# A decoder layer: shared expert cut at 384 and 320, and the output norm on ScalarE

## The reference

```python
yg = xf @ shared_gw.T
y, g = jnp.split(yg, 2, axis=-1)          # 704 hidden columns each
shared = jax.nn.silu(g) * y @ shared_dw.T
...
for e in range(N_EXPERTS):                # 8 experts, 352 hidden columns, top 2
    h = jax.nn.silu(g_e) * u_e
    out = out + h @ down_w[e].T * we[:, None]
x = _layernorm(x + shared + out)
```

## Time and profile before

| what | value |
|---|---|
| median of 3 runs | 1037.55 us (1037.47 to 1037.67) |
| the profiled execution | 1038.49 us |
| its span | 1036.8 us |
| PE busy | 1010.6 us, 97% of the span |
| DVE busy | 748.6 us, 72% |
| ACT, POOL busy | 566.4 us, 581.7 us |
| mean granted clock of TensorE | 0.998 |

### The profile page before, as it was taken

How to read it: one execution, slowest core, us unless ns; L and a number is a source line. 1 busy time by engine, 2 the same in 40 slices (tenths; PEclk the granted TensorE clock), 3 DMA queues, 4 the chain that set the end, 5 groups by cost and what they waited for, 6 DMA issues and landing times.

```text
span 1036.8 us, 20483 instructions
## 1 busy us (share of the span) xinstructions
PE 1010.6 (97%) x6817; PEld 905.3 (87%) x6817; DVE 748.6 (72%) x1567; ACT 566.4 (55%) x1221; POOL 581.7 (56%) x565
## 2 busy tenths in 40 slices
PE   8999999999999999999999999999999999999997
PEld 8866678999999999999999999999887888888885
DVE  4268876767767777777776776776786567789857
ACT  5355555655555565555555655555653347777610
POOL 1157777754744754744745745745564545555553
PEclk9999999999999999999999999999999999999999
DMA  8100104324333323233233233234220779999743
GB/s 283 82 22 12 61 22 156 147 115 152 120 110 113 105 107 115 100 111 116 97 114 112 98 119 105 97 125 134 102 89 2 272 281 387 402 403 403 296 122 112
DMA packets 45275, 153.48 MB, mean 148 GB/s; under 512 B 3768, under 2 KB 4792, under 8 KB 42144
## 3 DMA queue, kind: packets, MB, share of 16 engines
q1 hardware_dynamic: 42976, 145.38, 38.7%
q0 software_dynamic: 2240, 7.34, 2.2%
HBM read 130.04 MB, written 22.66 MB: 147 GB/s over the span
## 4 chain that ended last, share of the span: by engine, by line
PE 63%; POOL 8%; issue 5%; DVE 5%; ACT 2%; DMA 1%; POOLq 0%; DVEq 0%; ACTq 0%; SPq 0%
PE xa_y_ps L86 5%; PE xa_y_ps L88 5%; PE xa_y_ps L87 5%; PE xa_turn_ps L2123 3%; PE xa_turn_ps L2167 3%; PE ex_raw_gu_ps L86 3%; PE ex_raw_gu_ps L88 3%; PE ex_raw_gu_ps L87 3%; PE front_k_ps L86 3%; PE front_k_ps L88 3%; PE front_k_ps L87 3%; PE xa_turn_ps L2065 2%; PE xa_scores_ps L2153 2%; PE xa_scores_ps L2149 2%; PE ex_raw_ey_ps L2313 2%
## 5 line engine op out<-in xcount | busy, mean ns | idle before, releaser
L1646 DVE TENSOR_TENSOR xa_kT_lo<-xa_turn_ps,xa_kT_hi 128x750 fp32r<-128x750 f32 x63 | 59.1, 939 | 100.0 <-ACT xa_kT_hi L1427 100.0
L1326 POOL TENSOR_TENSOR xa_probs<-xa_probs,xa_inv_sum 112x750 f32<-112x750 f32 x63 | 94.8, 1505 | 63.3 <-DVE xa_inv_sum L1697 63.3
L1309 POOL TENSOR_TENSOR k_ms<-k_ss,sum_eps 125x6 f32<-125x6 f32 x63 | 12.6, 200 | 160.8 <-DVE k_ss L1662 160.8
L1443 ACT CAST xa_probsT<-xa_turn_ps 125x672 fp32r<-125x672 f32 x62 | 44.6, 720 | 86.4 <-PE xa_turn_ps L2167 86.4
L1312 POOL TENSOR_TENSOR k_inv<-k_ms,neg_half 125x6 f32<-125x6 f32 x63 | 83.6, 1328 | 8.3 <-POOL k_ms L1309 6.7
L1449 ACT ACTIVATE xa_probs<-xa_scores_ps,xa_bias,xa_q_scale 112x375 f32<-112x375 f32 x126 | 82.8, 662 | 7.0 <-DVE xa_bias L1672 5.5
L86 PE MATMUL front_k_ps<-land_xa_wk_hi,land_xa_ctx 128*125 128x256 f32 x252 | 71.8, 285 | 2.2 <-DVE front_k_hat L1689 1.8
L87 PE MATMUL front_k_ps<-land_xa_wk_hi,land_xa_ctx 128*125 128x256 f32 x252 | 70.8, 281 | 0.0
L88 PE MATMUL front_k_ps<-land_xa_wk_lo,land_xa_ctx 128*125 128x256 f32 x252 | 70.8, 281 | 0.0
L1423 ACT ACTIVATE front_k_sq<-front_k_ps 125x512 f32<-125x512 f32 x63 | 37.7, 599 | 60.2 <-PE front_k_ps L88 58.6
L423 POOL TENSOR_TENSOR sa_masked<-sa_masked,sa_row_max 112x448 f32<-112x448 f32 x32 | 30.2, 945 | 60.9 <-DVE sa_row_max L653 60.4
(11 more groups left out here) (445 smaller groups left out, 3703.6 us busy)
## 6 DMA issues: line engine op xcount, KB each, us to landing
xa_nat<-ctx_split SPq DMA_DIRECT2D x56, 750.0 KB
ex_raw_raw<-in_w_units SPq DMA_DIRECT2D x15, 1408.0 KB, 8.2
ex_raw_raw<-in_w_units SPq DMA_DIRECT2D x15, 768.0 KB, 8.1
land_ex_raw<-in_w_units SPq DMA_DIRECT2D x8, 1408.0 KB, 8.0
land_ex_raw<-in_w_units SPq DMA_DIRECT2D x8, 768.0 KB, 8.2
ctx_split<-xa_nat SPq DMA_DIRECT2D x8, 750.0 KB
sorted_x<-ex_raw_y_sb SPq DMA_DIRECT2D x7, 768.0 KB, 10.6
ex_raw_x_nat<-sorted_x SPq DMA_DIRECT2D x21, 256.0 KB, 8.4
```

The lines of the kernel that those rows point to most:

```text
L1326: pool.tensor_tensor(probs[0:T, u % 2], probs[0:T, u % 2], inv_sum[0:T, u % 2, :].unsqueeze(2).broadcast_to([T, 2, KV]), ALU.mult).then_in ...
L1646: dve.tensor_tensor(kT_lo[:, :, 0:KV], turn_ps[:, :, 0:KV], kT_hi[:, :, 0:KV].bitcast(F32), ALU.subtract).then_inc(sem["kT_lo_done"], 1)
```

## The change

Four things change.

1. The shared expert's 704 columns are cut at 384: unit A has 384 in three tiles of 128, unit B 320 in tiles of 128, 128 and 64. In unit B the last 64 gate columns and the last 64 up columns lie side by side in one stationary operand of 128, so steps k = 2 and k = 5 make one half with 12 matmuls, where 24 were. Gate comes out on partitions 0 to 63, up on 64 to 127; SiLU reads the first and writes the second, and the product, its two parts and the down weights of that tile lie on partitions 64 to 127.
2. Unit A's 768 up columns don't fit the 704 of the weight buffer. The last 128 are a tensor of their own, `w_third`: SP loads it (256 KB) behind the last query projection of cross attention, ACT makes its high part between two turned tiles, POOL its low part, and step k = 2 of unit A waits for that.
3. In the last steps on DVE, the last `hidden_low` stands ahead of the last two `combine`.
4. For output tiles 0 to 5 the normalisation leaves DVE. POOL makes mean times reciprocal root and its negative, two more instructions a tile, and ACT computes scale times x plus bias. Tile 6 stays on DVE. SP waits for ACT's semaphore for six tiles.

The core of the diff:

```diff
@@ dense_up @@
-                for half in range(2):
-                    w = slice(half * HID + at, half * HID + at + m)
+                if (base, c) == (0, HC - 1):
+                    pe.wait_ge(xs["third_up_lo"], 1)
+                for half in range(1 if base > 0 and c == HC - 1 else 2):
+                    w = slice((2 * c + half) * P, (2 * c + half + 1) * P)
                     for d in range(DC):
-                        mm = three_products(pe, gu_ps[0:m, n % 2, half, 0:HT], w_hi[:, d, w], w_lo[:, d, w],
+                        if (base, c, half) == (0, HC - 1, 1):
+                            st_hi, st_lo = third_hi[:, d, :], third_lo[:, d, :]
+                        else:
+                            st_hi, st_lo = w_hi[:, d, w], w_lo[:, d, w]
+                        mm = three_products(pe, gu_ps[:, n % 2, half, 0:HT], st_hi, st_lo,
@@ SP @@
+            sp.wait_ge(sem["q_ready"], 4 * PAIRS)
+            sp.dma_start(third_raw, w_third).then_inc(xs["third_up_loaded"], 16)
@@ ACT @@
             for t in (2, 3, 4):
                 turn_high(act, t)
+            act.wait_ge(xs["third_up_loaded"], 16)
+            act.copy(third_hi, third_raw).then_inc(xs["third_up_hi"], 1)
...
+            for t in range(TILES - 1):
+                act.wait_ge(xs["out_shifted"], 2 * t + 2)
+                act.activation(resid[:, t, :], resid[:, t, :], ACT.Identity, bias=total[:, 1, t:t + 1],
+                               scale=env["ln_rstd"][:, t:t + 1]).then_inc(xs["out_applied"], 1)
@@ POOL @@
             pool.memset(h_blk[:, HID:HPAD], 0.0).then_inc(xs["consts_set"], 1)
+            pool.wait_ge(xs["third_up_hi"], 1)
+            pool.wait_ge(norm["turn_lo"], TILES)
+            pool.tensor_tensor(third_lo, third_raw, third_hi.bitcast(F32), ALU.subtract).then_inc(xs["third_up_lo"], 1)
...
                 out_power(pool, t)
+                if t < TILES - 1:
+                    pool.wait_ge(xs["ln_pow"], t + 1)
+                    pool.tensor_tensor(total[:, 0, t:t + 1], env["ln_mv"][:, t, 0:1], env["ln_rstd"][:, t:t + 1],
+                                       ALU.mult).then_inc(xs["out_shifted"], 1)
+                    pool.wait_ge(xs["out_shifted"], 2 * t + 1)
+                    pool.tensor_tensor(total[:, 1, t:t + 1], env["zero"][:, 0:1], total[:, 0, t:t + 1],
+                                       ALU.subtract).then_inc(xs["out_shifted"], 1)
@@ DVE @@
                 if k == 3:
                     down_low(1, LAST_U)
+                if k == UPS - 1:
+                    hidden_low(1, UPS - 1)
                 for n in range(3 * k - 3, min(3 * k, GATHERS)):
                     combine(n)
-            hidden_low(1, UPS - 1)
             for t in range(TILES):
                 add_shared(t, TILES + NB)
                 dve.wait_ge(xs["y_taken"], TILES + NB + t + 1)
                 out_stat(dve, t)
-                if t >= 1:
-                    out_apply(dve, t - 1)
             out_apply(dve, TILES - 1)
```

More of the change, by code:

```diff
@@ L1489, in silu @@
                     act.wait_ge(xs["mul_done"], base + k - 1)
-                act.activation(silu_g[0:m, (base + k) % 2, :], gu_ps[0:m, (base + k) % 2, 0, 0:HT], ACT.Silu).then_inc(xs["silu_done"], 1)
+                act.activation(silu_g[rows, (base + k) % 2, :], gu_ps[0:P - rows.start, (base + k) % 2, 0, 0:HT], ACT.Silu).then_inc(xs["silu_done"], 1)
             def hidden_high(unit, k):
                 g, c = divmod(k, HC)
-                m = HID_TILES[c][1]
+                rows = rows_of(unit, c)
                 act.wait_ge(xs["mul_done"], k + 1 if unit == 0 else UPS + NB + k + 1)
@@ L1498, in hidden_high @@
                     act.wait_ge(xs["y_ready"], TILES)
-                act.copy(h_hi[0:m, c, g * HT:(g + 1) * HT], h_full[0:m, k % 2, :]).then_inc(xs["h_hi_done"], 1)
+                act.copy(h_hi[rows, c, g * HT:(g + 1) * HT], h_full[rows, k % 2, :]).then_inc(xs["h_hi_done"], 1)
             def third_high(j):
@@ L1798, in gated @@
             def gated(k, base):
-                m = HID_TILES[k % HC][1]
+                rows = rows_of(min(base, 1), k % HC)
                 n = base + k
@@ L1805, in gated @@
                     dve.wait_ge(xs["h_lo_done"], shared - 1)
-                dve.tensor_tensor(h_full[0:m, k % 2, :], silu_g[0:m, n % 2, :], gu_ps[0:m, n % 2, 1, 0:HT],
+                dve.tensor_tensor(h_full[rows, k % 2, :], silu_g[rows, n % 2, :], gu_ps[rows, n % 2, int(rows.start == 0), 0:HT],
                                   ALU.mult).then_inc(xs["mul_done"], 1)
@@ L2263, in dense_down @@
                 cols = slice(t * P, (t + 1) * P)
-                for c, (_, m) in enumerate(HID_TILES):
-                    w = slice(c * D, (c + 1) * D)
-                    mm = three_products(pe, bank, h_hi[0:m, c, cols], h_lo[0:m, c, cols],
-                                        down_hi[0:m, w], down_lo[0:m, w], c == 0, c == HC - 1)
+                for c in range(HC):
+                    w, rows = slice(c * D, (c + 1) * D), rows_of(unit, c)
+                    mm = three_products(pe, bank, h_hi[rows, c, cols], h_lo[rows, c, cols], down_hi[rows, w], down_lo[rows, w],
+                                        c == 0, c == HC - 1)
                 mm.then_inc(xs["y_ready"], 1)
@@ L2426, in _, with decoder_layer @@
                 dense_down(1, t, TILES + NB)
-def decoder_layer(nc, xT, x, ctxT, ctx_nat, wvT, w_quads, w_pairs, gains, gateT, gate_bias, w_units, out):
+def decoder_layer(nc, xT, x, ctxT, ctx_nat, wvT, w_quads, w_pairs, gains, gateT, gate_bias, w_units, w_third, out):
     sorted_x = nc.dram_tensor("sorted_x", (SLOT_TILES * P, D), F32, kind="Internal").ap()
@@ L2492, with interleaved @@
     units = [unit(a["L0_ffn_up_w"][e].T, a["L0_ffn_down_w"][e].T) for e in range(EXPERTS)]
-    for s in range(SHARED // HID):
-        rows = slice(s * HID, (s + 1) * HID)
-        gu = np.concatenate([shared_gw[SHARED:][rows], shared_gw[:SHARED][rows]], axis=0)
-        units.append(unit(gu.T, shared_dw.T[rows]))
+    gate_up = np.stack([shared_gw[SHARED:].T, shared_gw[:SHARED].T], axis=1)
+    def interleaved(rows):
+        return np.concatenate([gate_up[:, :, c:min(c + P, rows.stop)].reshape(D, -1) for c in range(rows.start, rows.stop, P)], axis=1)
+    blank = np.zeros((D, CHUNK - 5 * P), shared_gw.dtype)
+    first, last = interleaved(slice(0, FIRST_HID)), interleaved(slice(FIRST_HID, SHARED))
+    whole = FIRST_HID + 2 * P
+    last_down = np.concatenate([shared_dw.T[FIRST_HID:whole], np.zeros((HALF_P, D), shared_dw.dtype), shared_dw.T[whole:]], axis=0)
+    for up, down in ((first[:, :5 * P], shared_dw.T[:FIRST_HID]), (last, last_down)):
+        units.append(np.concatenate([chunks(np.concatenate([up, blank], axis=1)).reshape(P, -1), chunks(down).reshape(P, -1)], axis=1))
     arrays = {
@@ L2509 @@
         "w_units": np.stack(units),
+        "w_third": chunks(first[:, 5 * P:]),
     }
```

32 lines of the change are left out of this document (20 added, 12 removed).

## The result

The changed kernel took **1041.38 us** (median of 8 runs, 1038.94 to 1044.95); the kernel before, in the same job, 1037.63 (8 runs, 1037.28 to 1038.97). The ratio is 1.0036, 95% interval 1.0023 to 1.0049: slower by 3.75 us. The forecast was 1039.95 with a range up to 1041.2, so the direction held and the size was too small; the range missed the median by 0.2 us.

The account below looks back on a forecast made before the run. DVE and PE were taken as equally late at the end, both hanging on POOL's gathers. Order 0.2 + gathers 0.3 - POOL 0.2 + clock 2.1 = +2.4 us on the median of 1037.55: 1039.95 us, range 1037.6 to 1041.2.

Parts of the forecast that it names:

- the clock's loss: PE's last five output tiles: after idling, tile 2 starts at 1.2 GHz, 4.6 us slow, +2.1 us (bounds 0 and 2.8).
- the gathers: POOL's twelve gathers before the first output addition: the last comes later, +0.3 us (bounds -0.8 and +0.9).
- PE's 24 matmuls: Steps 2 and 5 lose 12 each: 4.9 us less work on PE, nothing off the end.
- The new order on DVE: DVE wants step 5's low part before the last two combines and waits for ACT: +0.2 us (bounds 0 and 0.2).
- walking through the order with the old lengths: Replaying POOL's gathers against DVE's instructions with the earlier trace's lengths: twelfth gather 0.1 to 0.6 us later.
- rival of faster gathers: Lighter DVE lets gathers finish up to 3.6 us sooner: 1035.35 us, decided if the twelfth lands before 1013.7; chance 0.06.
- My own sign of being wrong: The forecast is wrong if output tile 0 is added before 1018.5; the addition was expected near 1020.
- DVE without six normalisations: Output tiles 0 to 5: 2.6 us less DVE work, but DVE then waits for PE's tiles: 0.
- POOL at the end: Adding epsilon for the last tile takes 0.24 us, not 0.42, so the last normalisation comes sooner: -0.2 us.
- The separate 128 columns: Their load on SP, copy on ACT and subtraction on POOL fit in idle time or finish early enough: 0.
- My one row of 6.0 us: The earlier trace's start, where PE works from 2.72 but is slow until 8.70; used to size the slow clock.
- One of 64 + 64 costs what one of 128 does: Steps 2 and 5 on PE: a stationary operand of 64 + 64 columns costs no more than one of 128.

Follow-up runs that it names:

- the second job's chip: Chip of the second of three jobs of follow-up runs; the kernel before took 1038.26 us there (16 runs).
- the filled gap's profile: The changed kernel with 15 useless matmuls on PE between the last unit's second and third output tile: 1044.13 us, ratio 1.0022.

## Why the prediction was off

The wait, the gap and a fall of the clock came as foretold. What failed are three terms of the sum: the clock's loss, sized at 2.1 us with 2.8 as its bound, measured at 4.5; the down product over 64 rows, put at nothing, measured at 1.8; and the gathers, forecast at +0.3, measured at -1.4 together with the order. The errors of the last two, +1.8 and -1.9 (the order's +0.2 included), cancel, which was luck, so the clock carries the miss: in the median run, 3.75 us slower, +1.8, -1.4 and -0.2 leave some 3.5 for it. That is an estimate which takes the other terms to be the same in every run.

- **PE's 24 matmuls: right, and the heart of it.** They took nothing off the end; PE waited for DVE's first addition instead. With the wait removed the cut is worth 2.0 us by the medians (1035.15 against 1037.19; ratios 0.9971 and 0.9987).
- **The new order on DVE: +0.2 forecast, 0.04 measured** with the kernel before.
- **The gathers: the wrong sign.** +0.3 forecast, with -0.8 as bound. The twelfth was issued 1.10 us sooner after the first, and its data was 0.9 us sooner there (3.71 us after the issue for 4.63, by the chains): -2.0, of which DVE gave 0.6 back, -1.4 with the order. The step that failed was walking through the order with the old lengths: the gathers whose issues took 1.16 to 1.20 us before took 0.95, and the long one was 2.43 instead of 2.66. The rival of faster gathers was thus half right: the twelfth landed at 1014.3, which is 19.4 us after the first gather and, counted so, just the point where the rival was to decide (1013.7); yet the gap it was to shorten was long enough. My own sign of being wrong, tile 0 added before 1018.5, was missed only by what lies ahead of the first gather: counted from there, the addition came at 23.85 us against 24.23. Why exactly those issues became shorter was not isolated. It takes the new cut, and not fewer matmuls: the run with the old cut and the new order keeps 21.03 us, and the one with the new cut and 24 matmuls has 17.8. In that one DVE's subtraction started at 1013.25, after the last issue had begun at 1013.14, and none of the last eight issues took over 0.95 us, which speaks for when DVE's instructions fall.
- **DVE without six normalisations: 0, right** (1.0001, and the run with the norm back).
- **POOL at the end: -0.2, right** (-0.20; -0.22 with the kernel before). ACT needs 0.81 us a tile, not 0.6, with room to spare.
- **The separate 128 columns: 0, right** on the second job's chip, by the first gathers (993.73 to 994.19 with them, 994.17 without). On the slower chips it is open, as said above.
- **The clock: right in kind, +2.1 forecast, 4.5 measured** in the profiled execution. The fall came, but tile 2 did not start at 1.2 GHz: the fall began 1.1 us after its first matmul here, and between 1.1 before and 0.6 after it in the five other profiles that have one. My one row of 6.0 us was no measure for its length. Six profiles with an idle stretch of 3.0 to 4.3 us before tile 2 all have a fall, of 3.4, 3.4, 3.4, 6.8, 10.2 and 13.6 us; all eight with an idle stretch of 0 to 1.3 us there, the kernel before among them, have none between there and PE's last matmul. At 0.46 us a slow microsecond that is a loss of 1.6 to 6.3 us, and I had taken 2.8 for the upper bound. The eight runs of the result show the same spread: the three fastest (1038.94 to 1039.38) have a mean granted clock of 0.997, the slowest (1044.95) 0.992 (though 0.991 stands at 1043.64), and 0.005 of 1042 us is 10.4 us more at half clock, or 4.8 us of time.
- **The term that was missing: the 64 rows.** "One of 64 + 64 costs what one of 128 does" was true of the stationary operand with 64 + 64 columns. I did not price the down product, whose third piece now lies on partitions 64 to 127. It costs 0.4 us a tile, 1.8 us at the end, and is avoided at no cost by taking the zero rows along. The Trainium skill (TensorEngine Tiling (Array Packing), Tiling Modes, Key Properties) says that changing the tiling mode drains TensorE. The rows fit that: 96 rows cost nothing extra (2.09 us a tile in the earlier trace rows), 64 cost 0.10 us at the change and once more right behind it. That a drain is the cause no run shows.

By terms: forecast 0.2 + 0.3 - 0.2 + 2.1 = +2.4; in the profiled execution -1.4 (gathers and order), +1.8 (rows), +4.5 (clock), -0.2 (root), +4.7. The length of the fall decided it.

## What to carry to other kernels

Matmuls cut ahead of a wait are worth nothing, and can cost: here TensorE, idle for 3.0 us or more ahead of tile 2, fell to half its clock each time, and the next stretch, in which it was the bound, paid for it; look for the buffer it waits for (here four free banks) before cutting its work, and if there is none, try to fill the gap. Price a change of layout in every product that reads it, not only in the one it was made for: a contraction over 64 partitions between ones over 128 took 0.4 us for each round trip. And a term that gives nothing now (the norm on ScalarE) can be worth 2 us once the wait beside it is gone, so try the parts together with the cure, not alone.

## What was not expected of the hardware

- The fall of the clock had no fixed length: between 3.4 and 13.6 us after gaps of 3.0 to 4.3 us, in kernels that are alike up to that point. The longest came with 3.91 us of idling, while 4.27 gave 6.8 and 3.51 gave 3.4.
- A long gap is not the whole of it. Of the eight idle stretches of 2.6 to 3.1 us at about 841 us, those of 2.73 and 3.06 us (the filled gap's profile, and the one with 24 matmuls and 128 rows) were followed by a fall of 3.4 us; two others of 3.06 (the changed kernel again, and the one with the norm back on VectorE) were not. The falls at about 768 us, in two profiles, had no idle stretch of 1.2 us or more before them, only many short ones.
- Matmuls over 64 partitions among those over 128 are 0.10 us apart more at each change and behind it; that makes four of a tile's nine distances 0.33 us in place of 0.23.
- 15 matmuls without a use, in the place of idling, kept the clock at 1.00 and brought the seventh addition from 43.32 to 37.79 us after the first gather, beside a profile with the longest fall; the median was 2.3 us lower.
- The same program takes 4 us more on some chips. With the new cut there are waits of ACT of up to 8.2 us there that no engine of the core is seen to end. Both stay open.
